# Edge counts of a graph layer by two 64-row array tiles in place of one 98-column product, and a last block that ends without GpSimd's drain

## The reference, cut to what matters

```python
x = x + gnn(layernorm(x), edge_index, W, b, resW, resb)
x = x + ffn(layernorm(x)[None], ...)[0]        # 6 experts, the 2 best for each node
# gnn: src and dst are the edges and a loop at each node
deg = segment_sum(ones, dst);  dis = rsqrt(deg);  norm = dis[src] * dis[dst]
for l in range(2):
    msg = norm[:, None] * (x @ W[l])[src]
    agg = segment_sum(msg, dst) + b[l]
    x = relu(agg + x @ resW + resb)
```

## Time and profile before

| | |
|---|---|
| Time, median of 3 runs | 1869.71 us (1867.43 to 1871.58) |
| The profiled execution | 1870.38 us |
| Its span, first to last instruction | 1865.4 us |
| TensorE's granted clock, mean | 0.990 of full speed |
| Busy | PE 96%, PEld 59%, DVE 60%, ACT 45%, POOL 18% |
| 0 to 182 us | preparation, messages, counts of pair 0 |
| 182 to about 940 us | first layer: sums, with counts of the next pair |
| 940 to about 1500 us | second layer: sums, counts loaded |
| 1500 to 1865 us | experts and the end |

### The profile page before, as it was taken

One profiled execution on the slowest core, in us unless ns is written; L12 is line 12 of the kernel. 1 busy time (PEld: TensorE's weight loads), 2 busy tenths in 40 slices (PEclk: granted clock), 3 DMA queues, 4 the chain that ended last, 5 costly groups with the idle time before them and its releaser, 6 DMA issues. The chain is left out here.

```text
span 1865.4 us, 35178 instructions
## 1 busy us (share of the span) xinstructions
PE 1794.0 (96%) x11072; PEld 1107.3 (59%) x11072; DVE 1118.9 (60%) x2813; ACT 847.2 (45%) x1822; POOL 342.8 (18%) x347
## 2 busy tenths in 40 slices
PE   4898999999999999999999999999999999999996
PEld 3676555555555555555544444444444488888885
DVE  7887667666666666666524444444444568555553
ACT  2467656555555565656512222222222232665562
POOL 1681000000000000000001111111111123333332
PEclk9999999999999999999999999999999999999998
DMA  7375988889889998999475555455555489224441
GB/s 221 101 133 99 339 295 318 299 316 304 281 264 323 276 323 323 331 350 324 159 306 184 183 187 184 183 183 183 184 184 196 182 268 325 85 81 127 135 143 51
DMA packets 135979, 416.70 MB, mean 223 GB/s; under 512 B 13686, under 2 KB 81612, under 8 KB 129641
## 3 DMA queue, kind: packets, MB, share of 16 engines
q1 hardware_dynamic: 90376, 255.13, 39.1%
q0 software_dynamic: 45392, 160.65, 27.9%
q10 hardware_dynamic: 144, 0.13, 0.0%
HBM read 162.27 MB, written 262.07 MB: 227 GB/s over the span
## 5 line engine op out<-in xcount | busy, mean ns | idle before, releaser
L1472 PE MATMUL bank<-parts,counts 128*128 128x512 f16 x4704 | 1153.8, 379 | 2.8 <-DVE counts L1594 2.8
L1472 PEld LDWEIGHTS bank<-parts,counts 128*128 128x128 f16 x4704 | 416.1, 97 | 360.4 <-DVE counts L1594 3.2
L1638 ACT ACTIVATE counts<-bank 128x392 f16<-128x392 f32 x768 | 376.2, 497 | 278.1 <-PE bank L1541 265.5
L629 DVE TENSOR_TENSOR rows<-rows,iota_lo 128x2048 bf16<-128x2048 bf16 x192 | 234.9, 1224 | 179.8 <-PE bank L1541 175.2
L1541 PEld LDWEIGHTS bank<-rows 128*128 128x128 bf16 x3072 | 220.7, 98 | 186.7 <-issue 26.8
L1541 PE MATMUL bank<-rows 128*128 128x98 bf16 x3072 | 267.5, 208 | 0.0
L629 DVE TENSOR_TENSOR rows<-rows,iota_hi 128x1568 bf16<-128x1568 bf16 x192 | 186.0, 969 | 0.0
L467 POOL DMA_INDIRECT first_rows<-route_rows,route_spot_i x49 | 47.9, 977 | 553.6 <-DVE tokens L458 394.4
L1487 ACT ACTIVATE middle<-bank 128x256 f32<-128x256 f32 x98 | 37.5, 382 | 184.5 <-PE bank L1472 170.4
L2269 PE MATMUL bank<-y_t,counts 128*128 128x256 f32 x480 | 115.1, 383 | 3.1 <-ACT y_t L2341 3.1
L2269 PE MATMUL bank<-h_t,counts 128*128 128x256 f32 x480 | 113.7, 380 | 0.0
(11 more groups left out here) (278 smaller groups left out, 1778.6 us busy)
## 6 DMA issues: line engine op xcount, KB each, us to landing
counts_table<-counts SPq DMA_DIRECT2D x25, 3136.0 KB, 15.4
counts<-counts_table SPq DMA_DIRECT2D x24, 3136.0 KB, 12.2
first_rows<-zero_rows POOLq DMA_DIRECT2D x3, 10530.0 KB, 58.0
second_rows<-zero_rows POOLq DMA_DIRECT2D x3, 10449.0 KB, 66.2
first_out<-zero_rows POOLq DMA_DIRECT2D x3, 10368.0 KB, 51.0
res_tile<-res_table SPq DMA_DIRECT2D x98, 128.0 KB, 2.7
first_rows<-zero_rows POOLq DMA_DIRECT2D x1, 10270.0 KB, 58.0
second_rows<-zero_rows POOLq DMA_DIRECT2D x1, 10191.0 KB, 62.2
```

The costliest lines, as they stand in the source:

```text
L629: return nc.vector.tensor_tensor(rows, k, v, ALU.is_equal)
L1472: mm = nc.tensor.matmul(acc[:, 0:2 * dim], counts[:, b, s, o * P:(o + 1) * P], parts[:, s, :], start=s == 0, stop=s == tiles - 1)
L1638: nc.scalar.activation(counts[:, b, :, :].rearrange("p s (o n) -> p o s n", o=2)[:, :, :, q * QUAD:(q + 1) * QUAD], bank[4 + q % 4][:, 0:Q ...
```

## The change

The counts of the two destination tiles of a pair are no longer one matmul on all 128 rows. They are two matmuls of 64 rows each, of 128x49, one on the array's rows 0 to 63 and one on rows 64 to 127 (in the built program tile size 64 by 128, positions 0 and 64), to two different banks. Eight node positions make a run: 16 matmuls, 392 columns in each of the two banks. One run takes the place of two quads, and `build` is called for even q alone. It waits until both banks of the run before the last one were copied. No units are held back at the end of a pair. ScalarE still makes 32 copies of 392 columns a pair, each now for one destination tile. The second one-hot matrix has 49 values in place of 98, so `iota_hi` and the shift of odd keys go away. In the first block a run uses both of the two banks, so it waits for both copies of the run before it. The last block is opened with `no_gpsimd_drain=True`.

```diff
-        QUAD = 4
-        quads = P // QUAD
+        RUN = 8
+        quads = 2 * P // RUN
...
+        def quad_nodes(q):
+            return slice(q % 2 * P + q // 2 * RUN, q % 2 * P + (q // 2 + 1) * RUN)
+
+        def count_nodes(lo, hi, u0, even_bank, odd_bank):
+            for u in range(RUN):
+                i, j = divmod(u0 + u, 2)
+                for o, out in ((0, even_bank), (1, odd_bank)):
+                    rows = slice(o * HALF, (o + 1) * HALF)
+                    mm = nc.tensor.matmul(out[:, u * tiles:(u + 1) * tiles], lo[rows, i, :, j], hi[rows, i, :, j], start=True, stop=True)
+                    if u == RUN - 1:
+                        mm.then_inc(quad_ready, 1)
...
-        pair_hi = sb("pair_hi", [P, 2, STEP // 2, width, 2], BF16)
+        pair_hi = sb("pair_hi", [P, 2, STEP // 2, tiles, 2], BF16)
...
                     if q >= 2:
-                        pe.wait_ge(quad_out, q - 1)
-                    for u in range(QUAD):
-                        at = (u0 + u) // 2
-                        mm = nc.tensor.matmul(quad_bank(q)[:, u * width:(u + 1) * width], lo_rows[r % ROW_BUFS][:, at, :, u % 2],
-                                              hi_rows[r % ROW_BUFS][:, at, :, u % 2], start=True, stop=True)
-                    mm.then_inc(quad_ready, 1)
+                        pe.wait_ge(quad_out, q)
+                    count_nodes(lo_rows[r % ROW_BUFS], hi_rows[r % ROW_BUFS], u0, quad_bank(q), quad_bank(q + 1))
...
-                    pe.wait_ge(quad_out, i * quads + (q - 3))
-                    for u in range(QUAD):
-                        at = (u0 + u) // 2
-                        mm = nc.tensor.matmul(bank[4 + q % 4][:, u * width:(u + 1) * width], rows_lo[:, r % 2, at, :, u % 2],
-                                              rows_hi[:, r % 2, at, :, u % 2], start=True, stop=True)
-                    mm.then_inc(quad_ready, 1)
+                    pe.wait_ge(quad_out, i * quads + (q - 2))
+                    count_nodes(rows_lo[:, r % 2, :, :, :], rows_hi[:, r % 2, :, :, :], q // 2 * RUN % STEP, bank[4 + q % 4], bank[5 + q % 4])
...
-                    spread = units - ahead - (0 if last else UNITS_AFTER_COUNTS)
...
-                        if not last:
+                        if not last and q % 2 == 0:
                             build(q, i + 1)
-                        to = units if q == quads - 1 else ahead + (q + 1) * spread // quads
-                        sum_units(pe, b, i, ahead + q * spread // quads, to, update.sums_out, update.sums_ready, first,
+                        sum_units(pe, b, i, ahead + q * (units - ahead) // quads, ahead + (q + 1) * (units - ahead) // quads, update.sums_out, update.sums_ready, first,
...
-                    onehot_rows(rows_hi[:, r % 2, :, :, :], keys[:, b, 0, nodes_of], iota_hi, STEP, width).then_inc(onehots_made, 1)
+                    onehot_rows(rows_hi[:, r % 2, :, :, :], keys[:, b, 0, nodes_of], iota_lo, STEP, tiles).then_inc(onehots_made, 1)
...
-            with nc.Block() as block:
+            with nc.Block(no_gpsimd_drain=True) as block:
```

More of the change, by code:

```diff
@@ L509, in gnn_moe_kernel @@
     slots = 64
-    width = 2 * tiles
+    HALF = P // 2
     assert router_h == P and dim == 2 * P and tiles % 2 == 1
@@ L608, in rows_of @@
             return table.rearrange("(t p) d -> p t d", p=P)
-        QUAD = 4
-        quads = P // QUAD
+        RUN = 8
+        quads = 2 * P // RUN
         STEP = 16
         steps = P // STEP
-        per_step = STEP // QUAD
+        per_step = 2 * STEP // RUN
         open_scope()
@@ L671, in gnn_moe_kernel @@
         pair_lo = sb("pair_lo", [P, 2, STEP // 2, P, 2], BF16)
-        pair_hi = sb("pair_hi", [P, 2, STEP // 2, width, 2], BF16)
+        pair_hi = sb("pair_hi", [P, 2, STEP // 2, tiles, 2], BF16)
         def rows_in(flat, values):
             return flat.bitcast(BF16).rearrange("p (i v j) -> p i v j", v=values, j=2)
-        lo_words, hi_words = STEP * P // 2, STEP * width // 2
+        lo_words, hi_words = STEP * P // 2, STEP * tiles // 2
         assert 2 * hi_words <= cols and lo_words <= cols
@@ L680, in gnn_moe_kernel @@
                    onehot_hi[:, :, :, :, :].rearrange("p b i v j -> p (b i v j)")[:, 0:2 * lo_words].rearrange("p (i v j) -> p i v j", v=P, j=2)]
-        hi_rows = [pair_hi[:, 0, :, :, :], pair_hi[:, 1, :, :, :], rows_in(src_sb[:, 0:hi_words], width), rows_in(src_sb[:, hi_words:2 * hi_words], width)]
+        hi_rows = [pair_hi[:, 0, :, :, :], pair_hi[:, 1, :, :, :], rows_in(src_sb[:, 0:hi_words], tiles), rows_in(src_sb[:, hi_words:2 * hi_words], tiles)]
         windows = onehot_lo[:, :, :, :, :].rearrange("p b s v j -> p (b s v j)").bitcast(I32)[:, 0:2 * pairs * slots].rearrange("p (t s) -> p t s", s=slots)
@@ L841, in _ @@
                 link(nc.gpsimd.iota(node[:, :], [[P, 2 * pairs]], 0, 1, allow_small_or_imprecise_dtypes=True))
[L843 to L846, removed]
+                nc.gpsimd.tensor_scalar(node_base[:, :], node[:, :], float(P), None, ALU.mult).then_inc(consts_made, 1)
                 link(nc.gpsimd.tensor_copy(ident_h[:, :], ident[:, :]))
@@ L921, in quad_copy @@
                     nc.scalar.activation(
-                        counts[:, 0, :, :].rearrange("p s (o n) -> p o s n", o=2)[:, :, :, q * QUAD:(q + 1) * QUAD],
-                        quad_bank(q)[:, 0:QUAD * width].rearrange("p (n o s) -> p o s n", o=2, s=tiles), ACT.Copy).then_inc(quad_out, 1)
+                        counts[:, 0, :, quad_nodes(q)],
+                        quad_bank(q)[:, 0:RUN * tiles].rearrange("p (n s) -> p s n", s=tiles), ACT.Copy).then_inc(quad_out, 1)
                 act.wait_ge(cleared, 4)
@@ L1005, in turn_keys, with count_run @@
                     tr.then_inc(keys_turned, 1)
-                def count_quad(q):
-                    r, u0 = divmod(q * QUAD, STEP)
+                def count_run(q):
+                    r, u0 = divmod(q // 2 * RUN, STEP)
                     if u0 == 0:
@@ L1051, in _ @@
                     for q in quads_after(t):
-                        count_quad(q)
+                        if q % 2 == 0:
+                            count_run(q)
             @block.vector
@@ L1215, in pair_tiles @@
                 def pair_tiles(r):
-                    onehot_rows(hi_rows[r % ROW_BUFS], keys_t[:, 0, 0, r * STEP:(r + 1) * STEP], iota_hi, STEP, width).then_inc(onehots_made, 1)
+                    onehot_rows(hi_rows[r % ROW_BUFS], keys_t[:, 0, 0, r * STEP:(r + 1) * STEP], iota_lo, STEP, tiles).then_inc(onehots_made, 1)
                 dve.wait_ge(dst_loaded, 16 * 3)
@@ L1459, in gnn_moe_kernel @@
         LAST_UNITS = tiles
-        UNITS_AFTER_COUNTS = 6
         SUMS_AHEAD = 12
@@ L1525, in count_and_sum @@
             rows_lo = carve([P, 2, STEP // 2, P, 2], BF16)
-            rows_hi = carve([P, 2, STEP // 2, width, 2], BF16)
+            rows_hi = carve([P, 2, STEP // 2, tiles, 2], BF16)
             def there(T):
@@ L1533, in build @@
                 def build(q, i):
[L1535 to L1536 removed]
+                    r = q // per_step
+                    if q % per_step == 0:
                         pe.wait_ge(onehots_made, i * steps + (r + 1))
[L1538 to L1543 removed]
+                    pe.wait_ge(quad_out, i * quads + (q - 2))
+                    count_nodes(rows_lo[:, r % 2, :, :, :], rows_hi[:, r % 2, :, :, :], q // 2 * RUN % STEP, bank[4 + q % 4], bank[5 + q % 4])
                 def sum_pair(i, b, first, last=False):
@@ L1638, in quad @@
                     nc.scalar.activation(
-                        counts[:, b, :, :].rearrange("p s (o n) -> p o s n", o=2)[:, :, :, q * QUAD:(q + 1) * QUAD],
-                        bank[4 + q % 4][:, 0:QUAD * width].rearrange("p (n o s) -> p o s n", o=2, s=tiles), ACT.Copy).then_inc(quad_out, 1)
+                        counts[:, b, :, quad_nodes(q)],
+                        bank[4 + q % 4][:, 0:RUN * tiles].rearrange("p (n s) -> p s n", s=tiles), ACT.Copy).then_inc(quad_out, 1)
                 def middle_sums(i, o):
```

2 lines of the change are left out of this document (removed).

## The result

The changed kernel takes 1889.52 us (1885.04 to 1892.44, 4 runs), the one before 1870.13 us beside it. The ratio is 1.0103, 95% interval 1.0079 to 1.0128: slower by 1%, inside the range and on the other side of the forecast of 1825 us. The profiled execution took 1888.13 us with a span of 1885.5. One execution of a later kernel, of 2623 us at a mean granted clock of 0.655, is left out of that kernel's ratio.

A forecast was written before the change was run, and what follows sets the result against it. TensorE's own list was taken to bound the first layer. From the profiled 1870.4 us: - 62.6 (count work) + 20.7 (shape changes) + 4.8 (pair ends) + 0 (first block) - 8.4 (drain) = 1824.9, say 1825 us; range 1800 to 1950.

The forecast's parts named there:

- What it does around a run: Entering and leaving each first-layer run: 768 changes of array shape at 0.027 us, a bare weight load, +20.7 us.
- count work, two tiles side by side: First-layer runs: two tiles work at once, 27 ns a node position, 0.217 us a run, -62.6 us over 384 runs.
- end of a pair: First layer: two copies and the loops outlast seven units, a new 0.20 us wait for 24 pairs, +4.8 us.
- first block: VectorE's shorter second comparison against waits for both banks in the first block: 0, with 2 us to either side.
- GpSimd's drain: End of the last block: without the drain the program ends 8.4 us sooner, -8.4 us.
- TensorE sets the pace of this stage: First layer: PE busy 756.60 of 758 us, so cheaper count matmuls win time one for one.
- nothing is lost inside a pair: First layer: a run's wait for the copies of the run before the last costs nothing, 2.0 us under 2.8.
- the first: Rival: TensorE runs empty at each change of shape, 0.188 us each, 144.4 us in all, 1948.6 us; chance 0.27.
- The second rival: First-layer runs: tiles take turns, 16 matmuls at 0.027 us, +20.7 us in place of the gain, 1908.2 us; chance 0.12.

The follow-up runs named there:

- halved: Changed kernel with two runs back to back, 32 matmuls for 16 node positions, 384 changes of shape in place of 768: 1859.81 us, ratio 0.9944 to the kernel before.
- doubled: Changed kernel with each first-layer run cut into two halves of four positions, 1536 changes of shape in place of 768: 1982.72 us in one run.
- one tile: Changed kernel with both matmuls of each node position on the array's rows 0 to 63: 1962.88 us in one run.
- the order alone: Kernel before with its 128-row, 98-column matmuls issued in the changed kernel's order, drain in: 1871.36 us, ratio 1.0008.
- runs with drain: Changed kernel with GpSimd's drain at the end of the last block back in: 1894.42 us, ratio 1.0141 to the kernel before.
- full rows: Changed kernel with all 16 matmuls of a run on 128 rows, no change of shape, same number of instructions: 1886.04 us in one run.

## Why the prediction was wrong

The mechanism of the gain was right and one term was mis-sized: the step "What it does around a run", where I took 0.027 us a change of shape, the bare weight load, "nearest to what rows show of neighbouring matmuls". Measured is 0.107. I had given 0.086 as the price at which the gain is gone.

| term | forecast, us | measured, us | from |
|---|---|---|---|
| count work, two tiles side by side | -62.6 | about -62 | 16 starts in 0.205 us, unit pitch as before |
| 768 changes of shape | +20.7 | about +82 | 0.10 out and 0.11 in, 384 times; 0.105 each when halved and when doubled |
| end of a pair | +4.8 | +1.2 | 0.05 us, 24 times |
| first block | 0 | +1.6, not clear of the spread | first store at 183.8, not 182.2 |
| GpSimd's drain | -8.4 | -7.3 and -7.4 | two measurements without it; 8.4 in the trace |

The first layer's terms give 21 of its 25.0 us. Some 2 us of the rest is my reading of a quad as 0.19 us, when two decimals allow 0.187, twice a run: 384 x 0.006. About 1 of the last 2 us lies in the units: in the single records the third and later units of a group go at 215.8 ns, the first two at 215.0, and the groups are now twice as long. I can't assign the rest. The 1.6 us of the first block is no measured effect: the first store came between 180.5 and 184.2 us in the other kernels with the old matmuls, and between 180.0 and 187.7 in those that share the changed block. VectorE's comparisons there did get shorter (556 ns, forecast 560), and in the same part TensorE waits up to 0.7 us for ScalarE's copies at single runs.

Point by point. That TensorE sets the pace of this stage held: every change of its list there came through one for one, until the seam. Side by side held, shown by the 0.205 us against 0.40 on one tile. That nothing is lost inside a pair held, and the order alone is worth 0.1% (0.0 to 0.2). The end of a pair came to 0.05 us and not 0.20 because of the price that I had missed: the way out and the way in, 0.10 and 0.11 us, cover the same copies and loops as the units do, and where they cost nothing the wait is 0.22 us. That this agrees with 0.20 has luck in it, since two readings were off in opposite directions, the copies (0.89 us, not 1.00) and the restart (0.23, not 0.06). The drain came within 1.1 us.

Of the rivals, the first was the one that decided, though not at its full price: I had drawn it as an engine that runs fully empty, 0.188 us, and it is a little more than half of that. The Trainium skill, "TensorEngine Tiling (Array Packing)", section "Key Properties", says that changing the mode drains the TensorE. By that rule the change had to cost something at every run, and the trace agrees with 0.107 us. I had weighed it at 0.27, and the Trainium skill has no time for it; what I should have taken from it is that the cheapest reading, a weight load that can't go ahead, leaves out every sort of emptying, so the value belonged between 0.027 and 0.188. The middle, 0.107, gives 1886 us; that it meets the measured price so closely is chance, since no row of the trace before gave it. The second rival, tiles that take turns, is excluded.

The Trainium skill, "TensorE: Matmul & The Clock Gate", section "Packing small matmuls: row/col tiling", says that tiles start some 4 ns apart. The single records of this trace agree, with 3 ns between the two starts of a node position. From one position to the next it is 27 ns, and 40 ns from the first to the second.

## What to carry to other kernels

Two 64-row tiles halve the time of small matmuls (49 columns here), and each change between these and 128-row matmuls costs about 0.1 us on TensorE, so the run between two changes must save more than 0.21 us: here eight positions save 0.16 and lose, sixteen save 0.32 and win. When a trace has no row for an operation and the bounds lie on both sides of the break-even, the sign isn't known, and a point forecast from the end that resembles the neighbours claims more than the trace shows. A bound engine that becomes faster brings its later transfers forward into others' traffic: look at the seams between stages before counting the gain. And when an engine is late, follow the chain of waits back to its start: here the late thing that stood out, the scatter, came 23 us after the wait that it was blamed for.

## What the runs showed of the hardware

- A change from 128-row to 64-row matmuls and back costs 0.107 us each way on average (0.11 in, 0.10 out), with units of 512 columns ahead or with fp32 transposes (0.10 there), and with one tile in use about as with two (0.08 out).
- Two 64-row tiles start their matmuls 3 ns apart and go on at 27 ns a pair, the same 27 ns that one 49-column matmul takes on 128 rows.
- GpSimd's drain at a block's end took 8399 ns in three programs alike (before, and the runs with drain and with full rows).
- Loads of 128 KB took 7.2 us to land in the median (up to 9.6) while a 10 MB store of zeros ran beside them, and 2.1 us (up to 2.7) with the store in eleven pieces.
